# Two-block attention and mixture-of-experts kernel: other engine order around router and results, a last store in three pieces, and one fp32 value made by ACT

## What is computed

```python
x = x + attention(group_norm(x))     # 12 heads of 32, 7x7 neighbourhood + 16 register keys
x = x + experts(group_norm(x))       # 4 experts, hidden 96, best 2 of 4

# experts, per token
probs = softmax(x @ router_w.T + router_b)
combine = top 2 of probs, divided by their sum (+ 1e-8), 0 for the others
hmid = gelu(x @ fc1_w.T + fc1_b)                       # 4 x 96
out = (hmid * combine) @ fc2_w + combine @ fc2_b
```

## Time and profile before

| | us |
|---|---|
| median of 3 runs | 669.32 (665.61 to 669.46) |
| the profiled execution's own time | 667.93 |
| its span, first to last instruction | 666.1 |
| PE busy in the span | 577.0 (87%) |
| DVE busy | 458.8 (69%) |
| ACT busy | 302.0 (45%) |
| POOL busy | 282.0 (42%) |
| mean granted TensorE clock | 0.974 of full speed |

### The profile page before, as it was taken

The page is one execution under the profiler, slowest core; times in us unless marked ns, Lnnn a source line. Parts: engine busy times, 40 slices in busy tenths (PEclk is TensorE's granted clock), DMA queues, the critical chain, the costliest instruction groups (busy, mean ns, idle before and its releaser), DMA issues.

```text
span 666.1 us, 22415 instructions
## 1 busy us (share of the span) xinstructions
PE 577.0 (87%) x9227; PEld 402.4 (60%) x9227; DVE 458.8 (69%) x1033; ACT 302.0 (45%) x597; POOL 282.0 (42%) x421
## 2 busy tenths in 40 slices
PE   3577778998899987998999988999769888997997
PEld 3336656677665765667775767657556445564554
DVE  5885455776887789875767768877779776772232
ACT  1762445315544288413553155442856528544321
POOL 3116688255222655336992552226626212213131
PEclk9999689999999999998999998999979999998999
DMA  9769594796339952497519964199530010110112
GB/s 301 185 148 292 146 194 150 190 271 184 103 73 222 262 151 65 108 244 217 146 46 220 254 170 137 40 253 253 153 96 25 1 36 36 71 38 35 72 52 91
DMA packets 131565, 95.44 MB, mean 143 GB/s; under 512 B 67292, under 2 KB 125320, under 8 KB 131464
## 3 DMA queue, kind: packets, MB, share of 16 engines
q1 hardware_dynamic: 121960, 75.18, 44.1%
q0 software_dynamic: 9504, 18.84, 9.2%
HBM read 57.62 MB, written 35.54 MB: 140 GB/s over the span
## 4 chain that ended last, share of the span: by engine, by line
PE 52%; DVE 20%; DMA 9%; SPq 7%; issue 6%; ACT 4%; POOL 2%; ACTq 0%; DVEq 0%; POOLq 0%
PE ps L1052 38%; SPq L272 5%; PE ps L1215 5%; PE ps L1166 4%; DVE MX L555 4%; DMA KB<-kscr 3%; PE ps L1192 3%; DVE GT_ L487 2%; DVE ST L448 2%; DMA vscr<-VT 2%; DVE SUMT L568 1%; DMA kscr<-KT 1%; DVE RINV L574 1%; DVE KT L525 1%; DMA VR<-vscr 1%
## 5 line engine op out<-in xcount | busy, mean ns | idle before, releaser
L555 DVE TENSOR_REDUCE MX<-ps 128x2 f32<-128x372 f32 x216 | 108.2, 540 | 68.7 <-PE ps L1166 67.7
L1052 PE MATMUL ps<-XH,WQ 128*128 128x384 f16 x810 | 143.4, 332 | 7.9 <-DVE XH L497 7.0
L1052 PEld LDWEIGHTS ps<-XH,WQ 128*128 128x128 f16 x810 | 78.4, 99 | 63.8 <-ACT XH L818 7.1
L877 ACT ACTIVATE PT<-ps 128x448 f32<-128x448 f32 (+1 forms) x162 | 78.6, 511 | 57.2 <-PE ps L1192 56.3
L1166 PE MATMUL ps<-KB,QS 120*32 120x186 f16 x1728 | 58.7, 253 | 24.1 <-DMA KB<-kscr 10.3
L1192 PE MATMUL ps<-QS,KB 122*128 122x112 f16 (+1 forms) x864 | 65.3, 216 | 14.4 <-ACT PT L877 9.0
L427 POOL TENSOR_TENSOR KT<-QS,KT 128x384 f16<-128x384 f32 x36 | 32.7, 918 | 106.3 <-ACT KT L966 106.3
L1052 PE MATMUL ps<-WQ,XH 128*128 128x128 f16 x972 | 63.5, 224 | 5.3 <-issue 5.0
L1192 PEld LDWEIGHTS ps<-QS,KB 122*128 122x128 f16 x864 | 44.4, 101 | 35.7 <-ACT PT L877 18.3
L374 POOL DMA_DIRECT2D QS<-MT x72 | 38.1, 534 | 61.3 <-ACT MT L867 61.2
L1052 PEld LDWEIGHTS ps<-WQ,XH 128*128 128x128 f16 x972 | 56.7, 100 | 11.4 <-issue 9.1
(11 more groups left out here) (167 smaller groups left out, 972.9 us busy)
## 6 DMA issues: line engine op xcount, KB each, us to landing
KB<-kscr SPq DMA_DIRECT2D x108, 192.0 KB, 7.3
kscr<-KT SPq DMA_DIRECT2D x72, 192.0 KB, 2.5
VR<-vscr SPq DMA_DIRECT2D x216, 56.0 KB
QS<-qscr SPq DMA_DIRECT2D x108, 96.0 KB, 6.0
out<-X SPq DMA_DIRECT2D x12, 576.0 KB, 3.3
X<-in_x SPq DMA_DIRECT2D x6, 576.0 KB, 7.3
qscr<-QT POOLq DMA_DIRECT2D x18, 192.0 KB, 3.3
qscr<-PT POOLq DMA_DIRECT2D x18, 192.0 KB, 5.3
```

What stands on the lines that cost most here:

```text
L555: V.tensor_reduce(out=MX[:, s % 2, t, 2 * pair:2 * pair + 2], in_=ps[:, S_BANK(s, i), 0:2 * RUN].rearrange("p (h n) -> p h n", h=2), op=AL ...
L877: A(PTS[n % 4][:, 0:w], ps[:, ST_BANK(n), 0:w], ACT.Exp, scale=SCORE).then_inc(s_["exd"], 1)
L1052: last = mm(bank, lhsT(a, k), rhs(b, k), start=(k == 0 and n == 0), stop=(finish and k == steps - 1 and n == 2))
```

## The change

- **Second weights' split** in stage 5 moves by a strip: ACT's L942 and L943 from s = 2 to s = 3, DVE's L507 from after s = 3 to after s = 4.
- **One of three fp32 values beside attention** (stages 2 and 5, chunk k = 2) is made by ACT at a = 3, no longer by DVE at a = 4. ACT waits there for all POOL low halves of the blocks before (`gn_lo_p`); POOL's low half of k = 2 waits for ACT's value (`gn_ta`). Counts in `tmps` follow.
- **Zeroing**: POOL zeroes CS[0] first, then B2, then CS[1]; `router(0)` waits for the first alone, `router(1)` for both.
- **PE**: `spread(1)`, `hidden(4)`, `hidden(5)` stand ahead of the wait for the last projection and for B2's low half; at the change of image `hidden(22)` and `hidden(23)` stand ahead of `spread(7)`.
- **DVE**: statistics are grouped otherwise around `weigh(3)` to `weigh(5)` and the first results; `result(3)` goes ahead of `more_parameters(3)`; in slabs 3 and 4 each result goes one place forward, ahead of `last_values` and `last_lows`.
- **ACT**: `hidden_high(6)` and (7) stand ahead of `hidden(8)` and `deviation(3)`.
- **SP**: the last slab is stored in three pieces of 192 KB, each when its own result is in.

```diff
@@ -163,8 +163,7 @@
         def tmps(n, blk, k):
-            done = (0, 2 * STRIPS, 2 * STRIPS + GN_STEPS, 2 * STRIPS + 2 * GN_STEPS)[n]
-            return done + (2 if n in (0, 3) else KC) * blk + k + 1
+            return 2 * (n * STRIPS + blk) + k + 1
@@ -307,11 +306,16 @@
             for m in range(SLABS):
+                img, a = divmod(m, TILES)
+                if m == SLABS - 1:
+                    for j in range(KC):
+                        sp.wait_ge(s_["y_done"], KC * m + j + 1)
+                        sp.dma_start(out[img, :, j, a * SN:(a + 1) * SN], xs(img, j, a * SN, SN)).then_inc(s_["y_out"], 16)
+                    break
                 sp.wait_ge(s_["y_done"], KC * (m + 1))
-                img, a = divmod(m, TILES)
                 xi = X[:, img * KC * N:(img + 1) * KC * N].rearrange("p (k n) -> p k n", k=KC)
                 sp.dma_start(out[img, :, :, a * SN:(a + 1) * SN], xi[:, :, a * SN:(a + 1) * SN]).then_inc(s_["y_out"], 16)
-            sp.wait_ge(s_["y_out"], 16 * SLABS)
+            sp.wait_ge(s_["y_out"], 16 * (SLABS - 1 + KC))
@@ -331,7 +335,10 @@
             def low_half(n, blk, k):
-                pool.wait_ge(s_["gn_t"], tmps(n, blk, k))
+                if k == 2:
+                    pool.wait_ge(s_["gn_ta"], n * STRIPS + blk + 1)
+                else:
+                    pool.wait_ge(s_["gn_t"], tmps(n, blk, k))
                 pool.wait_ge(s_["gn_hi"], n * GN_STEPS + blk * KC + k + 1)
@@ -381,8 +388,8 @@
                 pool.wait_ge(s_["gn_hi"], (img + 1) * GN_STEPS)
-                pool.wait_ge(s_["gn_t"], tmps(3 * img // 2, STRIPS - 1, 1 if img == 0 else 2))
-                pool.wait_ge(s_["gn_ta"], STRIPS)
+                pool.wait_ge(s_["gn_t"], tmps(img, STRIPS - 1, 1))
+                pool.wait_ge(s_["gn_ta"], STRIPS * (img + 1))
                 pool.wait_ge(s_["obx"], 1)
@@ -426,11 +433,10 @@
-            pool.wait_ge(s_["v_mm"], 6 * STAGES)
+            pool.wait_ge(s_["pv"], 36 * STAGES)
+            nc.gpsimd.memset(CS[0], 0.0).then_inc(s_["csz"], 1)
             nc.gpsimd.memset(B2, 0.0).then_inc(s_["b2z"], 1)
-            pool.wait_ge(s_["pv"], 36 * STAGES)
-            for img in range(IMAGES):
-                nc.gpsimd.memset(CS[img], 0.0).then_inc(s_["csz"], 1)
+            nc.gpsimd.memset(CS[1], 0.0).then_inc(s_["csz"], 1)
             for m in range(SLABS):
@@ -490,8 +496,8 @@
                 dve.wait_ge(s_["gn_hi"], i + 1)
-                if n in (0, 3) and k == 2:
-                    dve.wait_ge(s_["gn_ta"], (0 if n == 0 else STRIPS) + blk + 1)
+                if k == 2:
+                    dve.wait_ge(s_["gn_ta"], n * STRIPS + blk + 1)
                 else:
@@ -654,9 +660,9 @@
                         if n:
-                            if a % 2 == 0:
+                            if a in (0, 2):
                                 normalised(n, s, a // 2)
-                            elif a // 2 not in POOL_K[n]:
+                            elif a % 2 and a // 2 not in POOL_K[n]:
                                 low_half(n, s, a // 2)
@@ -666,7 +672,7 @@
                         moe_weights_low(1, wr_flat, W1)
-                    if gi == 5 and s == 3:
+                    if gi == 5 and s == 4:
                         moe_weights_low(2, f2raw, W2)
@@ -736,7 +742,7 @@
             dve.wait_ge(s_["moe_in"], 32)
-            dve.wait_ge(s_["csz"], 2)
+            dve.wait_ge(s_["csz"], 1)
             router(0)
@@ -749,12 +755,18 @@
                                    op1=ALU.subtract).then_inc(s_["flo"], 1)
-            for k in range(KC):
-                weigh(KC + k)
-                last_statistics(6 + 2 * k)
-            for j in range(KC):
-                result(j)
-                last = last_statistics(12 + 2 * j)
+            weigh(3)
+            last_statistics(6)
+            last_statistics(8)
+            weigh(4)
+            last_statistics(10)
+            last_statistics(12)
+            weigh(5)
+            result(0)
+            last_statistics(14)
+            result(1)
+            last = last_statistics(16)
+            result(2)
             link(last)
@@ -762,8 +774,8 @@
             weigh(8)
+            result(3)
             more_parameters(3)
-            result(3)
             last_values(0)
@@ -775,10 +787,10 @@
                 weigh(3 * m + 2)
+                result(3 * m - 3)
                 last_values(blk + 1)
-                result(3 * m - 3)
+                result(3 * m - 2)
                 last_lows(blk + 1)
-                result(3 * m - 2)
                 result(3 * m - 1)
@@ -787,6 +799,7 @@
                 result(12 + j)
+            dve.wait_ge(s_["csz"], 2)
             router(1)
@@ -934,10 +947,14 @@
                             normalised(n, s, a // 2)
+                        if n and a == 3:
+                            if pool_lows(n, s) > 0:
+                                act.wait_ge(s_["gn_lo_p"], pool_lows(n, s))
+                            A(tmp_block(n, 2), x_block(n, s, 2), ACT.Identity, bias=cols["nb"][:, 2:3], scale=cols["rstd"][:, 2:3]).then_inc(s_["gn_ta"], 1)
                         if gi == 4 and s == 4 and a == 0:
...
                             A(W1.rearrange("p s k n -> p s (k n)")[:, 0], wr_flat, ACT.Copy, scale=WS).then_inc(s_["fhi"], 1)
-                        if gi == 5 and s == 2 and a == 5:
+                        if gi == 5 and s == 3 and a == 5:
                             act.wait_ge(s_["f_in"], 48)
@@ -989,11 +1006,12 @@
                 hidden_high(unit)
-            for unit in (6, 7, 8):
-                hidden(unit)
+            hidden(6)
+            hidden(7)
+            hidden_high(6)
+            hidden(8)
+            hidden_high(7)
             deviation(3)
-            hidden_high(6)
-            hidden_high(7)
             for k in range(KC):
@@ -1378,11 +1396,11 @@
             last_out(8, 18)
-            pe.wait_ge(s_["op_done"], 18 * STAGES)
-            pe.wait_ge(s_["flo"], 4)
             spread(1)
...
             hidden(5)
+            pe.wait_ge(s_["op_done"], 18 * STAGES)
+            pe.wait_ge(s_["flo"], 4)
             result(0)
@@ -1409,9 +1427,12 @@
             spread(6)
-            for m in range(7, SLABS):
-                if m > 7:
-                    hidden(KC * m)
+            hidden(22)
+            hidden(23)
+            spread(7)
+            result(6)
+            for m in range(8, SLABS):
+                hidden(KC * m)
                 spread(m)
...
                 hidden(KC * m + 2)
```

## The result

| | before | changed |
|---|---|---|
| median of 4 runs, us | 669.12 (665.61 to 669.46) | 651.99 (651.17 to 653.11) |
| the profiled execution's own time | 667.93 | 652.61 |
| its span | 666.1 | 650.8 |
| mean granted TensorE clock | 0.974 | 0.992 |

The ratio of the times is 0.9763 (95% interval 0.9728 to 0.9798): 2.4% faster. Forecast were 655.5 us in a range of 650.5 to 661.5.

The account below looks back on a forecast made before the run. PE, busy 87% of the span, was taken as the chain in the expert part, while three engines take turns in attention. Terms summed to -12.8 from 667.93, giving 655.1; 655.5 us was forecast, range 650.5 to 661.5.

Parts of the forecast that it names:

- The weight split: Stage 5: one strip later, ACT's wait of 4.28 us for the load goes whole; -4.3, bounds -4.7 and -1.9.
- The fp32 value on ACT: Stages 2 and 5: ACT's added work slightly outweighs DVE's relief; +0.5 per stage, +1.0 in all, bounds -4.7 and +7.1.
- Zeroing: DVE's router(0): with CS[0] alone ahead on POOL it starts earlier, then waits for the logits; -1.4, bounds -1.9 and -1.0.
- PE's order around result(0): Expert part: spread(1) no longer waits for DVE, result(0)'s bank waits 0.6 for 0.95; -1.7, bounds -2.2 and -0.7.
- result(3) and slabs 3 and 4: Expert part: PE's bank waits for late DVE results go; -1.1 and -1.2, bounds together 0 and -2.3.
- Change of image: After spread(6): PE idles 1.35 us instead of 3.56 and the clock stays up; -3.3, bounds -3.6 and -1.9.
- Last store: Kernel's end: of three pieces only 192 KB remain, landing after 2.5 us, not 3.3; -0.8, bounds -0.5 and -1.2.
- Loads take over: Rival, stage 5: strip 4 stands still up to 2.4 us for its values' loads; 657.9 us, chance 0.10.
- ACT exposed in full: Rival, stages 2 and 5: the moved value's whole price on ACT shows, +7.1 for +1.0; 661.6 us, chance 0.12.
- Expert gains half lost: Rival, expert part: each removed wait lets PE reach the next, half of 8.7 gone; 659.9 us, chance 0.14.
- DVE relief: Rival, stages 2 and 5: DVE's relief counts in full, -4.7 for +1.0; 649.8 us, chance 0.08.
- ACT stalls on POOL: Rival, attention: ACT's new wait at a = 3, cover 0.1 us, stalls; slower, 675 at 2.0 us each, chance 0.04.

Follow-up runs that it names:

- undo_value: Changed kernel with the third fp32 value of stages 2 and 5 back on DVE; 653.06 us, ratio 0.979.
- undo_zero: Changed kernel with POOL's old zeroing order (B2, CS[0], CS[1]) and DVE waiting for both CS buffers; 653.95 us, run once.
- undo_spread: Changed kernel with PE's spread(1), hidden(4), hidden(5) back behind the wait for the last projection; 656.52 us, run once.
- split_only: Kernel before with only the second weights' split moved one strip later; 657.95 us, ratio 0.9889.
- value_only: Kernel before with only the third fp32 value of stages 2 and 5 moved to ACT; 669.85 us, ratio 1.003.
- early_loads: Changed kernel, third fp32 value on DVE, second expert and router weights loaded ahead of stage 5's values, their high halves at strip 3, step 3; 651.47 us, ratio 0.9746.
- swap_filler: Changed kernel with PE's old order at the change of image and 18 unused products ahead of spread(7); 651.42 us, run once.

## Why the prediction was right

Point by point, in its order:

- **The weight split** (forecast -4.3, before the value's cost). Mechanism right: the wait is gone, the casts stay exposed (1.15 us in strip 3). The size is partly luck. Strips 2 and 3 went from 21.88 to 17.78 us, -4.1; but in five of the seven executions of this kind they took 16.5, which is -5.4, and the changed kernel's own profile has a strip 2 of 8.94 us where those have 7.69. So the term was about 1 us too small, and this profile's chance hid it. Alone the edit gave -4.8 in one profile, undone +3.0 in another. DVE's low halves one strip later cost nothing that can be seen.
- **The fp32 value on ACT** (+0.5 per stage). Stage 2 +0.83, and 0.5 to 0.9 by the strips of all profiles; stage 5 not settled by its total. The price is in other places than reckoned: 0.14, 0.39 and 0.36 us in strips 0, 1 and 5, where 1.1 was put on 0 and 5, and strip 1 was to hide it. That strip 1 grew is the sign which the prediction named as the worst; it was 0.1 to 0.4 us, and ACT's lists of waits show none for POOL in stages 2 and 5 of any profile. DVE's relief in strips 1 to 3, of which half was counted (0.7 per stage), is 0.02 and 0.05 us in strips 2 and 3. So the small net came from a smaller price and no relief, not from the two that were set off. The rows behind it: the twelve values that moved took 0.47 us each in before, 5.7 in all. The 24 that stayed kept their delay: above the undisturbed 0.474 us a value, DVE's values lost 26.9 - 36 x 0.474 = 9.8 us before and 22.6 - 24 x 0.474 = 11.2 after, and no value that overlapped no instruction of POOL took over 0.476 (timelines of DVE and POOL, both kernels). The Trainium skill (SBUF — State Buffer, Who interferes with whom) tells of a lock between DVE and POOL that ACT never meets; the trace agrees, since ACT's values kept 0.707 us, while the lock stays with the values left on DVE. The 9.0 us of saving that the prediction worked out from that rule did not come, since the moved values were none of the delayed ones. The price at the router, 0.3 us, was not in the sum.
- **Zeroing** (-1.4): the router came 1.22 earlier; with the value on DVE it would have been 1.52 (undo_value). What the step did not see is that the idle piece ahead of `combine(0)` was about to be long enough for the clock to fall. In before, PE ran `hidden(0)` and `hidden(1)` slowly (4.64 us) and that filled its idle time; in the changed kernel they took 3.08, and only 1.78 us of idle time remained. With the zeroing undone (undo_zero) it was 3.01, and 1.6 us more for the clock. The term was sized right against before, for a reason that was half luck.
- **PE's order around result(0)** (-1.7): -1.43 at `spread(1)` as written, and -0.73 behind it where 0.35 was reckoned; the bank's wait fell from 0.95 to 0.2, not to 0.6. Together that is -2.16, 0.5 more than forecast. undo_spread shows that 1.24 of it hang on PE's order, and leaves 0.92 to DVE's.
- **result(3) and slabs 3 and 4** (-1.1 and -1.2): -2.75 in all. The two waits of 0.61 came back to the hundredth when undone. The high halves' order was worth more than I wrote, 1.6, overlapping with the other.
- **Change of image** (-3.3): -3.24. Idle 1.33 us (forecast 1.35), clock 1.00 through it, as the step said from the pieces of 1.24 and 1.28.
- **Last store** (-0.8): -1.1. 192 KB landed after 1.9 us, faster than the 2.5 of the row that I took for it, a store of the same size to another place while the attention ran; which of the two made the difference is not shown.
- **The sum**: -12.8 forecast, -13.1 in the stretches that hold an edit. In the expert part, where single profiles repeat, this is a fair test: -10.5 against -9.5 forecast, with all terms' sizes within 0.5. In the two attention stages it is not: -2.6 against -3.3 forecast, in stages whose length varies by 1.3 to 2 us between executions of the same instructions. The two differences, 1.0 and 0.7, cancel. So the agreement to 0.3 us is finer than one pair of profiles can show, and is luck. (The change of image was -3.5 + 0.3, which is -3.2, not the -3.3 that went into the sum.) The forecast time was 3.5 us too high. Of this 2.2 lie in the two stretches without an edit, 0.3 in the terms, 0.4 in my choice of 655.5 over the sum's 655.1, and 0.6 in the new median, which lies that far below the new profiled execution.

**The slow `hidden(0)` and `hidden(1)`.** Why they ran slowly in before is open. PE had no idle piece in the 9 us ahead of them, but in the last 2.7 us only the short products of the logits, of 8 and 4 columns (windows, before, columns as in rows 4):

```profile
513.00:516.00 3.00, 3.00 (x111) 2.91 (x110) 2.19 (x5) 0.00 (x0) 2.97 (x4) 0.94 0.02 5
516.00:520.00 4.00, 4.00 (x17) 1.97 (x15) 2.47 (x8) 1.55 (x3) 1.26 (x1) 0.62 0.00 0
```

The same products ran slowly in split_only, value_only, undo_value and early_loads too, and at full speed in the other nine profiles. In all five slow ones PE waited for the router after them, 0.1 us in undo_value and early_loads and 1.4 in the others, so the slowness itself cost nothing.

**The stretches without an edit.** The start to stage 2's first exponential and stage 2's last output to stage 5's first exponential hold the same instructions in all fourteen profiled executions, but for the two loads that the early_loads kernels issue in the second. Together they took 428.1 us in before, 425.9 in the changed kernel, and 422.6 (swap_filler, split_only) to 429.9 (undo_value) in all: a span of 7.3 us, in which both lie. So the -2.2 can't be told from chance, and much of the spread of whole times lies there. What varies there I did not follow up; waits of PE for transfers (KB<-kscr, VR<-vscr) differ between the executions in number and length, but that they are the cause is only argued.

**The rivals.** Loads take over: not seen. ACT exposed in full: falls, 0.8 of up to 3.5 in stage 2. Expert gains half lost: falls, the parts kept all but 0.2 and 0.4. DVE relief: falls, value_only has none. ACT stalls on POOL: no such wait in the stages of any profile.

## What to carry to other kernels

On a chain of one engine that the waits name, price each wait from its row and check what stands next in both lists: in the expert part each group of terms priced so was within 0.5 us of what its stretch showed. In the attention, where three engines take turns and stretches vary by more than an edit is worth, look at strips and at several executions before calling a term right. Ask also which instructions of a group carry its delay: the mean of 0.753 us hid that the twelve which moved had none. When an idle piece of TensorE comes out of an order, look at its length, for it may cost as much again in clock; and a ready product put into it can be worth more than the wait itself. A whole-time comparison could tell none of the parts below 1% apart; cutting the profiles at the same events could, where the stretches repeat to 0.02 us as in the expert part.

## What the runs showed of the hardware

- An idle piece of 1.33 or 1.78 us left PE at the upper clock level (18 products in 3.09 to 3.10 us). Pieces of 3.01 and 3.56 us were followed by the lower one: 4.70 and 5.35 us for the same 18 products. The same piece of 3.56 us cost 1.0 us less in before (15.85 against 16.86 us from spread(6) to spread(8)), so what a long piece costs is not fixed.
- An idle piece is not needed for the lower level: in before the granted clock was 0.62 from 516 to 520 us, with PE busy all through the 6 us ahead of it, the last 2.7 with products of 8 and 4 columns alone; in the changed kernel it was 1.00 behind the same products. Why is open.
- 18 useless products in such a piece gave back 2.68 us, more than the order itself was worth (1.57).
- Moving a third of DVE's fp32 values away left the time lost beside POOL as it was (9.8 and 11.2 us): the moved ones had taken 0.47 us each, undisturbed.
